# Two gated expert layers on one core: the gate values worked out on VectorE after the first weight group instead of before it

## The reference, cut to what matters

```python
x = x + tanh(g_xattn[0]) * L0_xattn(ctx_1024, layernorm(x), mask, ...)
x = x + tanh(g_ffn[0])   * L0_ffn(layernorm(x), router_w, router_b, w1, w3, w2)   # 4 experts, hidden 2048
x = x + tanh(g_xattn[1]) * L1_xattn(layernorm(x), ctx_1024, ..., stride 16)
x = x + tanh(g_ffn[1])   * L1_ffn(layernorm(x), Wg, W1, W2, W3)                   # 8 experts, hidden 1024
```

## Time and profile before

| | us |
|---|---|
| median of 3 runs | 2025.17 (2024.57 to 2027.11) |
| the profiled execution, its time | 2012.94 |
| the profiled execution, its span | 2011.2 |
| TensorE busy | 1892.3 (94%) |
| VectorE busy | 1047.6 (52%) |
| ScalarE busy | 805.8 (40%) |
| GpSimd busy | 645.3 (32%) |

### The profile page before, as it was taken

One profiled execution on the slowest core, in us unless ns is written; L12 is line 12 of the kernel. 1 busy time (PEld: TensorE's weight loads), 2 busy tenths in 40 slices (PEclk: granted clock), 3 DMA queues, 4 the chain that ended last, 5 costly groups with the idle time before them and its releaser, 6 DMA issues. The chain is left out here.

```text
span 2011.2 us, 35308 instructions
## 1 busy us (share of the span) xinstructions
PE 1892.3 (94%) x12144; PEld 1541.4 (77%) x12144; DVE 1047.6 (52%) x2409; ACT 805.8 (40%) x1733; POOL 645.3 (32%) x520
## 2 busy tenths in 40 slices
PE   7999999999999999999599999999998867999994
PEld 4788787878878787878378888888875657899983
DVE  6536565655656565545553333233345756644564
ACT  4434343433334343433443334333314535555550
POOL 4030202002030302000045554355521205787872
PEclk9999999999999999999799999999998977999997
DMA  7731012121211221000333333223367034645546
GB/s 290 242 134 55 23 46 75 41 81 40 62 60 55 66 55 28 18 17 14 111 118 110 110 115 125 63 99 110 117 240 290 14 134 145 210 136 181 189 155 208
DMA packets 122363, 220.26 MB, mean 110 GB/s; under 512 B 41883, under 2 KB 46779, under 8 KB 120295
## 3 DMA queue, kind: packets, MB, share of 16 engines
q1 hardware_dynamic: 117415, 202.62, 30.1%
q0 software_dynamic: 4800, 15.73, 2.3%
HBM read 189.47 MB, written 28.03 MB: 108 GB/s over the span
## 5 line engine op out<-in xcount | busy, mean ns | idle before, releaser
L508 POOL TENSOR_TENSOR a_cols<-a_cols,a_moments_b 128x722 f32<-128x722 f32 x32 | 58.4, 1824 | 546.6 <-DMA a_moments_b<-a_moments_dram 518.2
L677 PE MATMUL a_kv_ps<-a_kvin_hi,a_wk_hi 128*128 128x512 f32 (+1 forms) x512 | 195.5, 382 | 0.0
L1176 PE MATMUL f_banks<-f_wab_hi,f_x_hi 128*128 x448 | 183.8, 410 | 0.7 <-DVE f_x_lo L1869 0.7
L678 PE MATMUL a_kv_ps<-a_kvin_lo,a_wk_hi 128*128 128x512 f32 (+1 forms) x512 | 179.6, 351 | 0.0
L679 PE MATMUL a_kv_ps<-a_kvin_hi,a_wk_lo 128*128 128x512 f32 (+1 forms) x512 | 179.6, 351 | 0.0
L1178 PE MATMUL f_banks<-f_wab_hi,f_x_lo 128*128 x448 | 176.8, 395 | 0.0
L1177 PE MATMUL f_banks<-f_wab_lo,f_x_hi 128*128 x448 | 176.1, 393 | 0.0
L1891 DVE TENSOR_TENSOR f_h_sb<-f_h_sb,f_banks 128x256 f32<-128x256 f32 x112 | 47.2, 421 | 240.4 <-ACT f_h_sb L1614 239.4
L589 ACT ACTIVATE a_probs<-a_probs,a_neg_max 100x822 f32<-100x822 f32 x128 | 126.0, 984 | 101.3 <-DVE a_neg_max L974 101.3
L1614 ACT ACTIVATE f_h_sb<-f_banks 128x256 f32<-128x256 f32 x112 | 43.1, 385 | 290.6 <-PE f_banks L1178 290.6
L677 PE MATMUL a_kv_ps<-a_wv_hi,a_kvin_hi 128*128 128x512 f32 (+1 forms) x384 | 156.7, 408 | 0.1
(11 more groups left out here) (426 smaller groups left out, 4797.0 us busy)
## 6 DMA issues: line engine op xcount, KB each, us to landing
f_raw<-f_pieces SPq DMA_DIRECT2D x94, 256.0 KB, 2.7
m_raw<-m_pieces SPq DMA_DIRECT2D x92, 256.0 KB, 3.0
f_wab_raw<-f_pieces SPq DMA_DIRECT2D x42, 512.0 KB, 6.1
m_wab_raw<-m_pieces SPq DMA_DIRECT2D x42, 512.0 KB, 6.2
a_rows<-ctx_rows SPq DMA_DIRECT2D x8, 1536.0 KB, 7.1
a_cols<-ctx_cols SPq DMA_DIRECT2D x8, 1444.0 KB, 7.5
ahead_piece<-g_ctx SPq DMA_DIRECT2D x2, 2880.0 KB, 18.5
a_moments_b<-a_moments_dram SPq DMA_DIRECT2D x7, 722.0 KB, 4.4
```

The costliest lines, as they stand in the source:

```text
L677: nc.tensor.matmul(out, hi_l, hi_r, start=first, stop=False)
L678: nc.tensor.matmul(out, hi_l, lo_r, start=False, stop=False)
L1176: nc.tensor.matmul(out, left_hi, right_hi, start=start, stop=False)
```

## The change

In the opening of `gated_experts` on VectorE, the read of the slot count and the whole of group 0 now come ahead of the gates; the gates come behind the last sum of group 0 and ahead of group 1. Both calls of the function (f_ and m_) are changed. No instruction is added or taken away, and no other engine's order changes.

```diff
                 if c == AHEAD + 5:
                     low_tokens(0, 1)
+            dve.wait_ge(expert_done, 2)
+            used = dve.value_load(expert[0:1, SLOTS:SLOTS + 1], min_val=0, max_val=SLOTS)
+            group(0, 0, True)
             dve.wait_ge(exp_done, 1)
             for k in range(TOP):
                 own.link(nc.vector.scalar_tensor_tensor(work[0:M, :, :], rank[0:M, :, :], float(k), p_exp[0:M, :, :], ALU.is_equal, ALU.mult))
...
             own.link(nc.vector.tensor_tensor(gates[0:M, :, :], gates[0:M, :, :], p_sum[0:M, :].unsqueeze(2).to_broadcast([M, B, TOP]), ALU.mult))
             dve.sem_inc(gates_done, 1)
-            dve.wait_ge(expert_done, 2)
-            used = dve.value_load(expert[0:1, SLOTS:SLOTS + 1], min_val=0, max_val=SLOTS)
-            for g in range(G):
-                group(0, g, g == 0)
+            for g in range(1, G):
+                group(0, g, False)
             with dve.If(used > CORE):
```

## The result

The changed kernel takes 2033.38 us in the median of 20 runs (2024.88 to 2040.34), the kernel before 2026.84 in 20 runs beside them (2022.03 to 2033.94). The ratio is 1.0031, 95% interval 1.002 to 1.0041: **slower by 4 to 8 us**, where 2026.4 was forecast, 1 us slower, with a range up to 2029.8.

What follows compares the result with a forecast made beforehand. TensorE was taken as the bound (busy 192.00 of 192.00 us in the second expert stage). -4.1 + 0 + 0 + 3.6 + 1.7 = +1.2 us on the 2025.17 median gives 2026.4; own range 2024.7 to 2028.8, wider range 2021.0 to 2029.8.

Steps and rivals of the forecast that it cites:

- Opening, m_ stage: -4.1: Second expert stage's start: gates leave VectorE's path, the count read goes ahead, TensorE never pauses; 4.1 us earlier, otherwise 3.4.
- rival B: Second stage's opening gives nothing back because GpSimd's gathered token rows end last; the new wait stays: +5.3, 2030.5 us, chance 0.07.
- The first step that failed: Sum made on the 2012.94 us profile, carried to the 2025.17 median, taking TensorE's boundness as independent of the 12 us between.
- Opening, f_ stage: 0: First expert stage's start: TensorE has no hole there, so 1.8 us less on VectorE are worth 0.
- Transition, f_ stage: 0: First stage, between groups 0 and 1: gates delay the product to 1082.8 at latest, TensorE's second slot covers it; cost 0.
- Transition, m_ stage: +3.6 and +1.7 for the clock: Second stage, groups 0 to 1: gates wait for GpSimd's running splits, TensorE late by 3.6 us; 3.4 us at half speed lose 1.7.
- the lower bound of 0.3: Second stage, groups 0 to 1: short gate instructions slip through beside GpSimd's splits, so TensorE is late by only 0.3 us.
- The second step that failed: Gates beside GpSimd, second stage: each two-SBUF-input instruction waits at most about one split, one every 1.26 us; gave the 3.6.

Runs made afterwards that it cites:

- e1: Changed order in the m_ stage alone, f_ stage as in the kernel before: 2020.64 us against 2017.87, ratio 1.001 (0.9997 to 1.0023).
- after: The profiled execution of the changed kernel, both stages changed against the kernel before: 2038.28 us, against 2012.94 for the profiled kernel before.
- e5: The changed kernel once more, for a second profile: 2033.51 us against 2027.53 for the kernel before, ratio 1.0016 (1.0001 to 1.0031).
- e6: Changed kernel, but all eight gate instructions inside group 0 where GpSimd has nothing to split: 2026.36 us against the kernel before's 2027.53, ratio 0.9992.
- e12: The same kernel as e6 once more, timed against the kernel before: 2028.25 us against 2026.18, ratio 1.0006 (0.9995 to 1.0017).
- e11: The changed kernel again, for a third profile, a single execution: 2034.92 us against 2026.18 for the kernel before.
- e15: The m_ stage alone changed, once more, against the kernel before: 2034.31 us against 2026.31, ratio 1.0033 (1.002 to 1.0046).
- e7: Changed kernel plus a GpSimd wait for the finished gates during group 1's splits, both stages: 2030.82 us against the kernel before's 2027.53, ratio 1.0008.
- e2: Changed order in the f_ stage alone, m_ stage as in the kernel before: 2018.78 us, ratio 1.0007 (0.9993 to 1.002).
- e10: Changed kernel with the gates computed again, results unused, behind groups 1 to 6 of both stages: 2071.47 us.
- e14: The same kernel as e3 once more, against the kernel before: 2028.17 us against 2026.31, ratio 1.0004 (0.999 to 1.0017).
- e8: Kernel before plus 76 trials behind its last stage, VectorE instructions with two SBUF inputs beside GpSimd runs of eight subtractions: some 900 us longer.
- e9: The kernel before, unchanged, profiled once more: 2028.86 us.
- e3: Changed kernel, but the eight gate instructions spread over slots 1 to 4 of group 0: 2014.97 us, ratio to the kernel before 0.9987 (0.9976 to 0.9998).

## Why the prediction was wrong

**Opening, m_ stage: -4.1.** Right as a mechanism, and right in size on the quick chip: 36.9 against 40.8 to 41.6 is -3.9 to -4.7, and in e1 TensorE pauses there for 0.56 us at most, with the granted clock at 1.00 from 1683.4 us on. The read went ahead of the splits (TENSOR_LOAD at 1681.1, with nine VectorE instructions ahead of its place still to begin). The page "TensorE: Matmul & The Clock Gate" of the Trainium skill (Architectural detail) gives VectorE a queue of eight instructions; the trace agrees with that, and that such a read goes ahead is what the trace shows. On the chips where the change was timed the term is -2.7 (after, e5, e6, e12) or 0 (e11, e15, e7), because there ScalarE stands still for 5.6 to 8.0 us until an instant that hardly moves with the gates. The stall ends 37.9 to 38.1 us behind the rank reduction in the eight profiles of openings of 48.1 us and more, whatever the order, and at 38.6 to 40.5 in the other four. This is rival B's shape, "the opening gives nothing back", by another cause than its token rows: ScalarE, not TensorE's input. The first step that failed is the sentence in which I carried the sum over to the median, "TensorE's boundness in these stages doesn't depend on the 12 us between them". About 7 us sat in the very opening that the change was to shorten (48.1 to 48.4 against 40.8 to 41.6).

**Opening, f_ stage: 0.** Not settled. From the first split token to the sixth product e2 took 22.9 us against 24.0, 1.1 gained; on the other chips the old order took 25.5 to 26.5 and the new one anything from 24.3 to 31.2.

**Transition, f_ stage: 0.** Right in price: the distance from the last copy to the second product is 5.86 to 5.88 us in every profile, of either order. The wait itself was not the forecast's: where the gates met GpSimd's run there, the first one waited until the run ended in all 11 cases (2.19 to 2.24 us in after, e2, e5 and e11, 2.67 to 2.68 in e10's seven), and not for the running split. TensorE's second slot covered it.

**Transition, m_ stage: +3.6 and +1.7 for the clock.** Without a lockout this is close. The first two waits ended with the running split (1.10 and 0.96 us in e11), the last one too (1.19); the product came 3.7 to 3.8 us later than before, and by group 2 it was 4.7 to 5.1 against the forecast's 5.3. TensorE itself waited 3.0 us (e1, e5, e11) where 3.6 was forecast, which leaves 1.7 to 2.1 us for the stretch behind it at a lower clock, where 1.7 was taken: e11 has 0.63 and then 0.87 there, with 17 and 27 matmuls in 3.4 us each, where full speed holds 32. The page "SBUF — State Buffer" of the Trainium skill (Who interferes with whom) was right against the lower bound of 0.3: instructions as small as 100x16 are blocked (1.19 us for 0.18). It speaks of one instruction of the other engine; the waits below span up to eight.

**The second step that failed** stands here, the sentence "The excess is at most about one GpSimd split: they wait for the running one to end". It holds in 8 of 12 m_ transitions (the 12 are one each in after, e1, e5, e11 and e15, and seven in e10). In 4 (after, two of e10's, e15) the first gate instruction waited out the whole run, 9.67 to 9.69 us, and the stage lost 11.7 to 12.4 us in place of 4.7 to 5.1. The earlier trace rows held no such case among 144 instructions, and the range had no room for it.

**A term that I did not have**: the same lockout of a weight split in the last group, worth 4.9 to 5.4 us at the end. It stands in 5 of the 11 profiles whose m_ opening has the changed order (e1, e5, e7, e14, e15) and in none of the 6 with the old one. That is no proof that the change brings it; the places are the same. The phase sorts them in part: the five began 0.634 to 0.655 us behind the start of a split; of the twelve that got in, eight began at 0.656 to 0.705 and only two, e8 and e11, at 0.638.

With these, on the other two chips: 0 to -2.7, +4.9, a third of 7 more, and up to half of 5.3 more, which is an estimate of 5 to 10 us, against 4 to 8 measured, and 4 to 9 in e15. The two shares are from a dozen profiles and rough. The 25.3 us between the two profiles shown are 7.0 ahead of the m_ stage, 4.1 in its opening, 1.4 in the rest of group 0, 12.4 at the transition and 0.4 behind it. Of the first, e1 has 5.4 too, whose code up to there is the old one, and e9, the kernel before itself, 7.7, so they are no part of the change.

What stays open: what in the full kernel makes a lockout possible, since none came in 136 trials by themselves, what decides between lockout and first gap, and what ScalarE waits for in the opening on two of the three chips.

**The best version measured** is e3 on the quick chip, 2.9 us under the kernel before (0.9987, 0.9976 to 0.9998); the changed kernel as a whole was not timed on that chip. On the others the gates spread (e14) and the gates late (e6, e12) are level with the kernel before, 5 to 7 us under the changed one by the medians (2026.4 to 2028.3 against e5's 2033.51 and e11's single 2034.92).

## What to carry to other kernels

Before a forecast from one profile is carried to a median 12 us away, find where those microseconds sit; here most of them sat in the stretch that the change was meant to shorten. A small VectorE instruction with two SBUF inputs is not small while GpSimd works through a run of such instructions: count on the running one each time, and on the whole run in some places and executions. If such work can wait, place it by GpSimd's idle stretches, not by VectorE's.

## What the runs showed of the hardware

VectorE's instruction of 100x64, 0.23 us by itself, took 9.67 to 9.69 us as the first gate instruction in 4 of 12 places and 1.07 to 1.28 us in the others, at much the same distance from GpSimd's instructions; that of 100x32 waited for the end of the run in all 11 places where one or two splits were left (2.19 to 2.68 us); a 128x512 subtraction took 8.56 us where its like took 1.2. In between there was nothing: either the first gap between GpSimd's instructions or the end of the run. In the 136 trials by themselves it was always the first gap, and the wait was what was left of the running instruction. An engine's read of a word into a register ran while nine of its instructions that stand ahead of it had not begun (1681.1 against 1686.84).
